# A two-layer hybrid network on one core: inverse roots spread by a stride-zero product, and the orders of the second attention and of layer 1 written anew

## The reference, cut to what matters

```python
x = x + L0_attn_a(_layernorm(x), ...)      # 32 heads, causal, rotary
x = x + L0_ffn(_layernorm(x), ...)         # 128 tokens chosen, attention and a gated product on them
x = x + L0_attn_b(_layernorm(x), ...)      # 16 heads of 128, causal: "the second attention"
x = x + L0_ffn(_layernorm(x), ...)
x = x + L1_attn_a(_layernorm(x), ...)      # gates and values, a linear recurrence
x = x + L1_ffn(_layernorm(x), ...)         # ternary weights, silu(up) * gate, down
x = x + L1_attn_b(_layernorm(x), ...)      # rms norm, conv, recurrence, rms norm, gelu product
x = x + L1_ffn(_layernorm(x), ...)

def _layernorm(x, axis=-1, eps=1e-05):
    m = jnp.mean(x, axis=axis, keepdims=True)
    v = jnp.var(x, axis=axis, keepdims=True)
    return (x - m) / jnp.sqrt(v + eps)

def _L0_attn_b_ref(x, W_Q, W_K, W_V, W_O, b_Q, b_K, b_V, b_O):
    q = jnp.einsum('bpd,hde->bphe', x, W_Q) + b_Q
    k = jnp.einsum('bpd,hde->bphe', x, W_K) + b_K
    v = jnp.einsum('bpd,hde->bphe', x, W_V) + b_V
    scores = jnp.einsum('bqhe,bkhe->bhqk', q, k) / ATTN_SCALE
    attn = jax.nn.softmax(jnp.where(causal, scores, IGNORE), axis=-1)
    z = jnp.einsum('bkhe,bhqk->bqhe', v, attn)
    return jnp.einsum('bqhe,hed->bqd', z, W_O) + b_O
```

## Time and profile before

| what | us |
|---|---|
| median of 3 runs | 1543.14 |
| lowest and highest | 1541.55, 1544.15 |
| the profiled execution, timed from outside | 1542.92 |
| its span in the trace | 1541.7 |
| PE busy | 1455.6 (94%) |
| DVE busy | 1131.5 (73%) |
| ACT busy | 1024.8 (66%) |
| POOL busy | 700.3 (45%) |

### The profile page before, as it was taken

The page is one execution under the profiler, slowest core; times in us unless marked ns, Lnnn a source line. Parts: engine busy times, 40 slices in busy tenths (PEclk is TensorE's granted clock), DMA queues, the critical chain, the costliest instruction groups (busy, mean ns, idle before and its releaser), DMA issues.

```text
span 1541.7 us, 23563 instructions
## 1 busy us (share of the span) xinstructions
PE 1455.6 (94%) x8388; PEld 1216.6 (79%) x8388; DVE 1131.5 (73%) x2487; ACT 1024.8 (66%) x2254; POOL 700.3 (45%) x820
## 2 busy tenths in 40 slices
PE   6999999999999998998999999999999977878898
PEld 5879888888889886786888888888886865655676
DVE  5888889889898975747766766766666659777646
ACT  3898989899898986445655655555554546464654
POOL 5758676666667563134423323323320512722233
PEclk8999999999999999999999999999999998988999
DMA  2000000000000001401000000000005031000000
...
DMA packets 14340, 45.12 MB, mean 29 GB/s; under 512 B 3216, under 2 KB 3216, under 8 KB 12048
## 3 DMA queue, kind: packets, MB, share of 16 engines
...
HBM read 42.55 MB, written 1.05 MB: 28 GB/s over the span
## 4 chain that ended last, share of the span: by engine, by line
PE 67%; DVE 18%; ACT 10%; issue 2%; POOL 1%; DMA 0%; SPq 0%; DVEq 0%; ACTq 0%; POOLq 0%
PE ps L149 27%; PE ps L348 14%; PE ps L1177 8%; PE ps L337 8%; DVE a_pT_lo L404 4%; DVE a_prob L357 3%; ACT a_pT_hi L396 2%; PE ps L1951 2%; PE ps L1957 2%; ACT a_prob L364 2%; DVE a_q L687 2%; ACT a_o_two L656 1%; PE ps L1967 1%; DVE f_r L1567 1%; PE ps L1970 1%
## 5 line engine op out<-in xcount | busy, mean ns | idle before, releaser
L379 POOL TENSOR_SCALAR a_prob<-a_prob,a_rowinv 128x128 f32<-128x128 f32 (+7 forms) x256 | 188.3, 748 | 109.0 <-DVE a_rowinv L373 108.4
L404 DVE TENSOR_TENSOR a_pT_lo<-ps,a_pT_hi 128x512 fp32r<-128x512 f32 (+3 forms) x384 | 195.8, 549 | 25.5 <-ACT a_pT_hi L396 22.5
L364 ACT ACTIVATE a_prob<-a_prob,a_negmax 128x128 f32<-128x128 f32 (+7 forms) x256 | 198.5, 782 | 9.2 <-DVE a_negmax L357 8.4
L379 POOL TENSOR_SCALAR b_prob<-b_prob,b_rowinv 128x128 f32<-128x128 f32 (+7 forms) x128 | 94.3, 749 | 234.6 <-DVE b_rowinv L373 234.6
L357 DVE CUSTOM_DVE_ANT_0 a_prob<-ps,a_mask 128x128 f32<-128x128 f32 (+7 forms) x256 | 188.0, 748 | 13.8 <-PE ps L149 13.5
L396 ACT ACTIVATE a_pT_hi<-ps 128x512 fp32r<-128x512 f32 (+3 forms) x384 | 169.1, 494 | 27.7 <-PE ps L348 15.1
L337 PE MATMUL ps<-ident,a_prob 128*128 128x128 f32 x1152 | 160.4, 275 | 6.8 <-DVE a_pT_lo L404 4.8
L364 ACT ACTIVATE b_prob<-b_prob,b_negmax 128x128 f32<-128x128 f32 (+7 forms) x128 | 99.7, 779 | 82.4 <-DVE b_negmax L357 82.1
L337 PEld LDWEIGHTS ps<-ident,a_prob 128*128 128x128 f32 x1152 | 130.8, 140 | 22.4 <-issue 8.2
L149 PE MATMUL ps<-a_k_hi,a_q 128*128 128x512 f32 (+3 forms) x384 | 140.5, 372 | 2.0 <-DVE a_negmax L357 1.2
L348 PE MATMUL ps<-a_pT_hi,a_v 128*128 128x512 f32 (+3 forms) x384 | 132.0, 351 | 2.4 <-ACT a_o_two L656 1.1
...
## 6 DMA issues: line engine op xcount, KB each, us to landing
...
```

The source lines that it names most:

```text
L364: act.activation(prob, prob, ACT.Exp, bias=a.negmax[:, n:n + 1], scale=-1.0, accum_out=a.rowsum[:, n:n + 1]).then_inc(*g.exped.mark(a.tag, u))
L379: pool.tensor_scalar(prob, prob, a.rowinv[:, n:n + 1], 1.0, ALU.mult, ALU.mult).then_inc(*g.normed.mark(a.tag, u))
L404: dve.tensor_tensor(lo, src, fr(hi), ALU.subtract).then_inc(*g.lo.mark(a.tag, u, j0 // 4))
```

## The change

It has three parts.

First, norms in the second attention and in layer 1 no longer build the diagonal. A new helper issues four products of 128 columns for each half. Each has as its weights one column of inverse roots, read 128 times with stride zero, and streams the identity:

```diff
+def spread_pe(g, pe, out, inv):
+
+    for j in range(HALF // P):
+        t = pe.matmul(out[:, j * P:j * P + P], inv[:, j:j + 1].broadcast_to([P, P]), g.ident[:], start=True, stop=True)
+    return t
...
     for b in range(NH2):
-        pe.wait_ge(*g.ndiag.at("b", b))
-        pe.matmul(g.bank[4 + b], g.ones[:], a.diag[:, b], start=True, stop=True).then_inc(*g.ninv.mark("b", b))
+        pe.wait_ge(*g.nrec.at("b", b))
+        spread_pe(g, pe, g.bank[4 + b], a.std[:, tiles_of(b)]).then_inc(*g.ninv.mark("b", b))
...
         dve.reciprocal(a.std[:, tt], a.std[:, tt]).then_inc(*g.nrec.mark("b", b))
-        dve.wait_ge(*g.nrec.at("b", b))
-        dve.tensor_tensor(a.diag[:, b].rearrange("p (j q) -> p j q", q=P), g.ident[:].unsqueeze(1).broadcast_to([P, HALF // P, P]),
-                          a.std[:, tt].unsqueeze(2).broadcast_to([P, HALF // P, P]), ALU.mult).then_inc(*g.ndiag.mark("b", b))
...
-    pe.wait_ge(*q.dve.at(tag, "diag"))
-    pe.matmul(q.bank[2], g.ones[:], q.diag[:], start=True, stop=True).then_inc(*q.pe.mark(tag, "inv"))
+    pe.wait_ge(*q.dve.at(tag, "rec"))
+    spread_pe(g, pe, q.bank[2], q.inv1 if tag == "l" else q.inv).then_inc(*q.pe.mark(tag, "inv"))
...
 def half_inverse_dve(g, dve, q, tag):
     dve.wait_ge(*q.act.at(tag, "std"))
     dve.reciprocal(q.inv[:], q.std[:]).then_inc(*q.dve.mark(tag, "rec"))
-    dve.wait_ge(*q.dve.at(tag, "rec"))
-    diagonal(g, dve, q.diag[:], q.inv[:]).then_inc(*q.dve.mark(tag, "diag"))
...
-    pe.wait_ge(*q.dve.at("l", "diag0"))
-    pe.matmul(q.bank[3], g.ones[:], q.sq[:, 0], start=True, stop=True).then_inc(*q.pe.mark("l", "inv0"))
+    spread_pe(g, pe, q.bank[3], q.inv).then_inc(*q.pe.mark("l", "inv0"))
...
-    dve.tensor_tensor(q.inv1[:], q.inv1[:], q.inv[:], ALU.mult).then_inc(*done.mark("l", "both"))
-    dve.wait_ge(*done.at("l", "both"))
-    diagonal(g, dve, q.diag[:], q.inv1[:]).then_inc(*done.mark("l", "diag"))
-    yield
-    diagonal(g, dve, q.sq[:, 0], q.inv[:]).then_inc(*done.mark("l", "diag0"))
+    dve.tensor_tensor(q.inv1[:], q.inv1[:], q.inv[:], ALU.mult).then_inc(*done.mark("l", "rec"))
```

Second, the four strings of the second attention are other strings with the same count of each letter; the start of PE's:

```diff
-    "qwqqqwssqqtssqqsswwttssqqttsqqsttsstvtsvsttssqqttsqqsttsstvtsvwswwttswsqqttsqqsttsstvtosvsttossqqttsqqsttossvttosvws"
+    "qwqqqwssqqstsqqssttwswsttqqttssqtqssvtvssttsstqqtsstqttqvsvtsswstwtswswsqttqstqsttsvqtssvototssqqsttsqtqosttsvsstovw"
```

54 lines of the change are left out of this document (30 added, 24 removed).

## The result

The changed kernel took 1527.74 us (1527.58 to 1528.15 in four runs), the kernel before 1543.18 (1541.55 to 1544.15): a ratio of 0.9913, 95% interval 0.9893 to 0.9933. Some of it is luck: three of these four runs of the kernel before lie above the median of the 110 timed later, 1541.6, and the changed kernel timed again beside 19 of them (e5) is 13.3 shorter. Both profiled executions had the same mean clock, 0.978 and 0.979.

The account below looks back on a forecast made before the run. The prediction took PE's instruction rate to bound the second attention, with cheaper DVE steps worth something in layer 1's middle stretches. Its terms summed to -5.8 from 1542.92, giving 1537.1, plus 0.2 for the median: 1537.3 us, range 1531 to 1543.5.

Parts of the forecast that it names:

- Attention, -0.4: Body of the second attention: same work, so new orders can only remove 0.9 us of PE waits; -0.4 taken.
- the sign of this error: Second attention: shortening by more than 1.5 us would mean the reading of its rate is wrong.
- Rival (a): Second attention: new orders bring bank handovers too close, PE waits on drains; +4.4 us, 1547.5; chance 0.11.
- Norm of the attention, -0.5: Second attention's norm: eight short records replace two long ones, so DVE goes on 0.16 to 0.98 us earlier; 0.5 taken.
- Norms of layer 1, -3.4: Layer 1: spreads cost PE the same as products by ones, and the 0.69 us diagonal goes where something waits; -3.4.
- norm l: Layer 1 norm, both halves: scaling comes earlier, the other half's operation lying beside the spread; 0.8 us twice, 1.6.
- norm r and t1's first half: First norms of layer 1: without the diagonal, DVE goes on earlier; gains 0.9 and 0.6 us.
- norm n2 of the second half: Late layer 1 norm: no gain, 0, because PE has other work ahead of the product.
- Orders of layer 1, -1.5: Layer 1: moved products fill PE's holes and freed DVE time is used; between -4.9 and +3.0, -1.5 us taken.
- The distance at norm l: Layer 1, sign of being right: reciprocal to scaling falls from 2.1 to about 1.1 us.
- the 57.2 for two heads: Second attention, sign of being right: the period for two heads stays 57.2 us.
- Rival (c): Norms: the spread is slower, its loads lying bare beside the passes; sum -0.5 us, 1542.6; chance 0.05.

Follow-up runs that it names:

- e4: Kernel before with PE's order alone changed at 26 places in the second attention: median 1549.4 us, ratio 1.0067.
- e7: Kernel before with one exchange of turns at 14 places of the second attention, alike on PE, DVE and ACT: median 1549.2 us, ratio 1.0046.
- e6: Changed kernel with the old layer 1 orders; new norms and new attention orders stay: median 1528.4 us, ratio 0.9926.
- e11: Kernel before with all new orders, attention and layer 1, but the old norms: median 1532.3 us, ratio 0.9954.
- e1: Kernel before with only the norms new, all orders old: median 1541.5 us, ratio 0.9994.
- e3: Kernel before with only the orders of layer 1 new; norms and attention orders old: median 1539.2 us, ratio 0.9991.
- e10: Changed kernel with a small unused DVE operation before each of 64 query and key drains in the second attention: median 1527.9 us, ratio 0.9926.

## Why the prediction was wrong, term by term

- **Attention, -0.4, was -5.5.** The step that failed is the sentence that the attention is at the rate at which PE takes instructions. I read the equal period of 57.18 for two heads as a rate; a chain of waits that repeats with the order has a period just as equal. And I took the list of PE's waits as complete. The text named the sign of this error (shorter by more than 1.5), and it came. Rival (a) had the right mechanism and the wrong side: I counted handovers by PE's work between them and found more close ones in the new strings. What counts is the whole chain with what is queued on ACT and DVE; by the drain's end against PE's start, 20 were tight before and one after. What new waits in this chain can cost, e4 and e7 show: +10.1 and +7.7.
- **Norm of the attention, -0.5, was 0.0.** The low-clock price was too low, 2.09 for what I put at 1.05 to 1.87.
- **Norms of layer 1, -3.4: right in size, by luck in its parts.** Free of the meeting, e6's layer 1 took 271.2 and e4's, with the old norms and orders, 275.4: -4.2; e11 against the changed kernel has -3.6, and the fastest runs of e1 and of before are 3.1 apart. At single norms the step that failed is norm l, where I had the other half's operation lie beside the spread: it waits for ACT, and 0.34 was to be had instead of 0.8. Of the -4.2, -0.5 lies up to t1 (1.5 forecast for norm r and t1's first half), -0.8 up to norm l of the first half (1.1), -1.7 in the stretch of both halves (0.8; the diagonal of n2 took 2.19 in e4 beside POOL's long operation, which I hadn't priced), and -1.5 at norm n2 of the second half and what follows, where I had put zero since PE had work ahead of the product. There the kernel before has down products at the low clock from 1452.8 to 1455.4, 0.43 apart; in the changed kernel the clock of that stretch is 1.00.
- **Orders of layer 1, -1.5, was -4.8 against the trace of before.** The step that failed is where the gain was looked for: holes of PE to be filled and freed DVE time to be used. By themselves, with no meeting to avoid, the new orders bring nothing: 274.0 for layer 1 in the changed kernel against 271.2 in e6, though at a lower clock in the stretch of both halves, 0.89 against 0.97. What they bring is that DVE's squares no longer start inside POOL's long operation, and they do so with the old norms too: in e3 and e11 the squares take 1.73 and 0.69, and layer 1 is 4.8 and 4.9 shorter than in the trace of before. That gain of about 5 was there to be read: 3.92 for an operation that takes 0.69 elsewhere. I looked at groups by mean. The new norms alone don't shut the meeting out as surely, by their times: eight of e1's runs take over 1541 and three of e6's over 1534. That those runs, and the kernel before above 1541 (61 of 110 runs), are this meeting is inferred from the times, since of e1 and e6 only runs at the short end (1530.8 and 1527.7) have a trace.
- **The sum** with measured terms: -0.8 ahead of the change, -5.5, and layer 1 -8.5, of which about -5 is the meeting and -3.5 the norms: -14.8, the difference of the two spans.
- **Signs.** DVE's busy time fell by 7.5 (8 to 10 forecast), the diagonal's line is gone, the records are 0.13 apart at 2.4 GHz. The distance at norm l, 3.01 to 2.67, did not come as forecast, nor did the 57.2 for two heads, with an attention 5.5 shorter. Rival (c) fell: 16 records with a load each took 2.05 at 2.4 GHz. By the Trainium skill ("TensorE: Matmul & The Clock Gate", "The mechanism") these loads, which use all rows, would lie bare; the trace disagrees.

The Trainium skill had the missing rule. "SBUF — State Buffer", under "Who interferes with whom", says that a DVE instruction with two SBUF inputs contends with a GpSimd instruction that reads SBUF, since its second input comes through the read interface they share, that this port pair is an exclusive lock, and that the order of issue decides who blocks. The traces agree: before, POOL is first and DVE's 3.92 ends with POOL's 3.75; in e10 DVE is first by 0.05 and takes 0.69, while POOL takes 3.94; and in pieces the wait is cut to one piece.
